# Index scratch in DRAM laid out by chunk, stored by groups of 32 partitions

## The reference, cut to what matters

```python
def _L0_ffn_ref(x, lut, gate_idx, up_idx, down_idx):   # lut: 16 values
    def _ghost_linear(x, idx, lut):
        w = lut[idx]
        return jnp.einsum('bsh,oh->bso', x, w)
    gate = _ghost_linear(x, gate_idx, lut)             # idx (1376, 512)
    up = _ghost_linear(x, up_idx, lut)                 # idx (1376, 512)
    h = jax.nn.silu(gate) * up
    return _ghost_linear(h, down_idx, lut)             # idx (512, 1376)
...
x = x + _L0_xattn_ref(_layernorm(x, axis=-1), ctx_1024, ...)
x = x + _L0_ffn_ref(_layernorm(x, axis=-1), L0_ffn_lut, ...)
```

## Time and profile before

| | |
|---|---|
| median of 3 executions | 803.66 us |
| the profiled execution | 803.88 us |
| its span | 802.1 us |
| TensorE busy | 752.2 us, 94% |
| VectorE busy | 518.6 us, 65% |
| ScalarE busy | 495.2 us, 62% |
| GpSimd busy | 265.2 us, 33% |
| moved by DMA | 61.49 MB in 75461 packets |

### The profile page before, as it was taken

How to read it: one execution, slowest core, us unless ns; L and a number is a source line. 1 busy time by engine, 2 the same in 40 slices (tenths; PEclk the granted TensorE clock), 3 DMA queues, 4 the chain that set the end, 5 groups by cost and what they waited for, 6 DMA issues and landing times.

```text
span 802.1 us, 14961 instructions
## 1 busy us (share of the span) xinstructions
PE 752.2 (94%) x5881; PEld 307.8 (38%) x5881; DVE 518.6 (65%) x1007; ACT 495.2 (62%) x1009; POOL 265.2 (33%) x276
## 2 busy tenths in 40 slices
PE   2887786999999999999999999999999999999998
PEld 1342232333443333224543332235433333265445
DVE  7979999899877994224879963228599810153221
ACT  3579889788556895662658866645489856511100
POOL 6883221000854322113843321035622310013320
PEclk9999999899999999999999999999999999999999
DMA  7649998596330000321400003222000000000001
GB/s 256 174 126 275 258 258 220 143 190 167 122 79 10 1 2 28 79 53 59 117 12 1 1 14 77 56 66 54 3 1 1 1 27 28 34 20 1 1 13 40
DMA packets 75461, 61.49 MB, mean 77 GB/s; under 512 B 34496, under 2 KB 61888, under 8 KB 75136
## 3 DMA queue, kind: packets, MB, share of 16 engines
q1 hardware_dynamic: 75056, 60.29, 28.3%
q10 hardware_dynamic: 208, 0.26, 0.1%
q0 software_dynamic: 128, 0.00, 0.0%
HBM read 43.55 MB, written 10.55 MB: 67 GB/s over the span
## 4 chain that ended last, share of the span: by engine, by line
PE 73%; DVE 16%; ACT 4%; issue 4%; POOL 3%; DVEq 0%; POOLq 0%; ACTq 0%
PE ps L1753 46%; PE ps L2120 8%; PE ps L2101 6%; PE ps L1819 5%; PE ps L2072 5%; DVE arena L1179 4%; DVE nmax L1548 3%; POOL hrstd L727 2%; ACT ps L1059 2%; PE ps L2107 2%; PE ps L1968 1%; DVE stat L1232 1%; DVE arena L1312 1%; DVE arena L1269 1%; DVE hvar L1302 1%
## 5 line engine op out<-in xcount | busy, mean ns | idle before, releaser
L1753 PE MATMUL ps<-arena,wf_hi 128*128 128x512 f16 (+1 forms) x704 | 201.4, 370 | 0.4 <-DVE arena L1192 0.4
L1059 ACT ACTIVATE ps<-ps,nmax 128x496 f32<-128x496 f32 x256 | 166.2, 652 | 23.1 <-DVE nmax L1553 23.1
L1091 ACT ACTIVATE arena<-ps 128x1024 f32<-128x1024 f32 x128 | 124.3, 1026 | 72.1 <-PE ps L2107 72.1
L1753 PE MATMUL ps<-arena,wf_lo 128*128 128x512 f16 (+1 forms) x352 | 130.0, 369 | 0.0
L1753 PE MATMUL ps<-wf_hi,arena 128*128 128x512 f16 (+3 forms) x374 | 114.8, 368 | 0.6 <-DVE arena L1196 0.6
L727 POOL TENSOR_TENSOR hrstd<-hvar,mhalf 128x16 f32<-128x16 f32 (+1 forms) x33 | 100.1, 3047 | 39.6 <-DVE hvar L1302 39.4
L1753 PEld LDWEIGHTS ps<-arena,wf_hi 128*128 128x128 f16 x704 | 64.7, 98 | 83.5 <-issue 20.5
L1179 DVE TENSOR_SCALAR arena<-arena,wf_lo 128x2048 f16<-128x2048 f16 (+1 forms) x132 | 89.6, 740 | 5.2 <-PE ps L1819 5.0
L1819 PE MATMUL ps<-arena,wf_lo 128*32 128x512 f16 (+1 forms) x1056 | 64.9, 389 | 13.0 <-ACT arena L886 9.6
L671 POOL TENSOR_TENSOR xrstd<-xvar,mhalf 128x1 f32<-128x1 f32 x32 | 24.0, 751 | 158.0 <-DVE xvar L1237 158.0
L1753 PE MATMUL ps<-wf_lo,arena 128*128 128x512 f16 (+3 forms) x187 | 68.5, 366 | 0.0
(11 more groups left out here) (164 smaller groups left out, 1051.6 us busy)
## 6 DMA issues: line engine op xcount, KB each, us to landing
arena<-idx SPq DMA_DIRECT2D x124, 128.0 KB, 3.5
arena<-in_x SPq DMA_DIRECT2D x32, 256.0 KB, 2.9
wf_lo<-in_idx SPq DMA_DIRECT2D x10, 512.0 KB, 5.1
idx<-wf_hi SPq DMA_DIRECT2D x10, 384.0 KB, 4.1
out<-arena SPq DMA_DIRECT2D x15, 256.0 KB, 2.0
wf_lo<-in_idx SPq DMA_DIRECT2D x11, 256.0 KB, 6.6
arena<-in_ctxT SPq DMA_DIRECT2D x5, 512.0 KB, 3.7
v_next<-arena SPq DMA_DIRECT2D x8, 256.0 KB, 4.2
```

The lines of the kernel that those rows point to most:

```text
L1059: last = act.activation(sc, sc, ACT.Exp, bias=nmax[:, 0, t, h:h + 1], accum_out=den[:, 0, t, h:h + 1])
L1091: act.activation(probs[n_ % 2][:, 2 * p:2 * p + 2, :], ps[:, bank:bank + 2, :], ACT.Exp).then_inc(s["probs_set"], 1)
L1753: last = pe.matmul(dst, l, r, start=(first and i == 0), stop=(stop and i == len(todo) - 1))
```

## The change

The scratch in DRAM becomes one flat array. Before, it had 128 rows, one for each partition, and a chunk was a column range of it, so that the four rows which one partition of a copy needs lay far apart: a piece of 1 KB each. Now a chunk is one range of the flat array, in the order k (32), g (4), column: what partition k of a copy needs is one piece of 4 KB (3 KB for the two short chunks). `load_rep` reads it so; it still issues four DMAs of 128 KB to 32 partitions each. For this the store must scatter: partition group g goes with one DMA of its own, in pieces of 1 KB that lie 4 KB apart. `store_idx` becomes 4 DMAs in place of 1 for blocks 1 to 10, and 8 in place of 1 for the short block, whose chunks have two widths. The first load of a block waits for all of them.

```diff
+def scratch_spans(it):
+
+    lo, mid, hi = block_at(it), down_at(it), block_at(it + 1)
+    return ((lo, mid, KQ * rows(it)), (mid, hi, D)) if it == SHORT else ((lo, hi, D),)
...
-        idx16 = nc.dram_tensor("idx16", (P, WCOLS), F16, kind="Internal").ap()
+        idx16 = nc.dram_tensor("idx16", (P * WCOLS,), F16, kind="Internal").ap()
...
             def store_idx(it):
-                cols = slice(block_at(it), block_at(it + 1))
                 sp.wait_ge(s["idx_16"], it + 1)
-                sp.dma_start(idx16[:, cols], wf_hi[:, cols]).then_inc(s[f"idx_out{it}"], 16)
+                for lo, hi, n in scratch_spans(it):
+                    for g in range(NR4):
+                        here = wf_hi[g * 32:(g + 1) * 32, lo:hi].rearrange("p (c n) -> p c n", n=n)
+                        there = idx16[P * lo:P * hi].rearrange("(c k g n) -> g k c n", k=32, g=NR4, n=n)[g]
+                        sp.dma_start(there, here).then_inc(s[f"idx_out{it}"], 16)
                 if it + STAGES < IT:
                     load_idx(it + STAGES)

             def load_rep(c):
                 lo, hi = CHUNKS[c]
                 if c % 3 == 0:
-                    sp.wait_ge(s[f"idx_out{c // 3}"], 16)
+                    sp.wait_ge(s[f"idx_out{c // 3}"], 16 * NR4 * len(scratch_spans(c // 3)))
...
-                src = idx16[:, lo:hi].rearrange("(g k) n -> k g n", g=NR4)
+                n = NR4 * (hi - lo)
+                src = idx16[P * lo:P * hi].rearrange("(k n) -> k n", k=32)
                 for r in range(NR4):
-                    dst = l_rep[c % REPS][r * 32:(r + 1) * 32, 0:NR4 * (hi - lo)].rearrange("p (g n) -> p g n", g=NR4)
-                    sp.dma_start(dst, src).then_inc(s[f"rep_in{c % REPS}"], 16)
+                    sp.dma_start(l_rep[c % REPS][r * 32:(r + 1) * 32, 0:NR4 * (hi - lo)], src).then_inc(s[f"rep_in{c % REPS}"], 16)
```

## The result

The changed kernel takes 805.42 us (median of 20 executions, 803.69 to 808.81), the kernel before 803.89 us in the same sessions (20, 802.47 to 806.49). The ratio is 1.0021, 95% interval 1.0013 to 1.0028: slower by 1.5 to 1.7 us, just at the size that I had called no change, and outside the range that I had given. The profiled execution took 806.06 us with a span of 804.2 us, 2.1 us more than the span before.

A forecast was written before the change was run, and what follows sets the result against it. The prediction took VectorE (58 to 142 us), then TensorE (to 204 us), as the bound, with DMA engines full but nobody waiting on the scratch. Its terms summed to 0, ends 0 and +0.5 us: 803.7 us, range 801.6 to 805.0.

The forecast's parts named there:

- the size that I had called no change: Whole run: differences up to about 0.2%, 1.6 us, count as no change; chance 0.82, own range 802.1 to 805.3 us.
- What bounds the kernel: Lookup, 58 to 204 us: VectorE until 142 us, then TensorE; DMA engines full, but only GpSimd waits for a DMA.
- The loads of 4 KB: The 132 replicated loads in 4 KB pieces: landing earlier gains 0 us, since nobody waits for them.
- the end "as now": Speed of the 4 KB loads: slow end, 2.65 us of DMA time a chunk, 198 GB/s; other end 1.39 us.
- The new wait for four stores: Chunk 3's load waits for block 1's four stores until 62.1 to 64.7 us; cost 0 us, 0.5 at the far end.
- The DMA engines' load: DMA time for two chunks: 7.6 to 11.05 us of 10.5; still hidden, share 0.72 to 1.0 from 58 to 142 us.
- the rival with a backlog: DMA engines fall behind, loads land late on VectorE in chunks 6 to 20: 11 us, 814.7 us; chance 0.05.
- The faster rival: Full DMA engines cost chain "issue" time from 58 to 142 us: 5.1 us would go, 798.6 us, half 801.1; chance 0.10.
- signs of being wrong: A DMA releasing the comparisons, chain "issue" shrinking by microseconds, or the comparisons' pace of 5.27 us a chunk moving.
- SP's additional stores: SP issues 37 more stores, 15.9 us, 1.3 us per two chunks in the loop; it fits, what queues behind is hidden.
- its second point: Index loads GpSimd waits for: conversion 5 moves from 81.83 to 83.1 us, ends at 84.6; hidden with 1.3 us left.
- My two slower rivals: DMA engines fall behind, 814.7 us, chance 0.05; chunk 3 starts late after its wait for stores, 805.5 us, chance 0.03.

The follow-up runs named there:

- one_store: Changed kernel with 4 KB loads, but host lays out index rows so each block is stored by one DMA of 128 partitions (two for the short block); 804.25 us, 1.0008.
- split_rows: Kernel before, old scratch and 1 KB loads, but each store issued as 4 DMAs of 32 partitions; 805.22 us, 1.0016.
- split_cols: Kernel before with each store issued as 4 DMAs, each a quarter of the columns on all 128 partitions; 805.67 us, 1.0029.
- idx_first: Changed kernel with the index load of block it + 2 issued before the four stores of block it instead of behind them; 804.32 us, 1.0008.
- conv5_inside: Kernel before, transfers untouched, but GpSimd's conversion 5 also waits for the first of the four comparisons of chunk 5; 805.83 us, 1.0033.
- conv5_behind: Changed kernel with GpSimd's conversion of block 5 put behind the two steps that followed it; 804.41 us, 1.0009.
- gated_after: Changed kernel with GpSimd's conversions of blocks 5, 9 and 10 moved to where VectorE compares nothing; 804.27 us, 1.0004.
- gated_idx_first: Changed kernel with the index load ahead of the stores and the conversions of blocks 5, 9 and 10 moved away from comparisons; 804.22 us, 0.9999.

## Why the prediction was wrong, by its own steps

**What bounds the kernel**: right. VectorE to 142 us and TensorE to 204 us are still the chain, and no comparison waits for a replicated load in the changed kernel. But from "the only engine that waits for a DMA is GpSimd" I drew that the transfer was slack. That wait was the one fed by SP.

**The loads of 4 KB**: right that nobody waits for them. As to speed the end "as now" held. In one_store, the loads of chunk 2 are alone between 42.5 and 46 us, as in the earlier trace rows; they ran at 204 GB/s against 198 with pieces of 1 KB:

```profile
42.50:46.00 3.50, 3.50 (x23) 2.37 (x23) 2.37 (x5) 2.94 (x6) 3.50 (x2) 1.00 0.88 204
```

So between the two rules of the Trainium skill, the one of "SBUF — State Buffer", Door 1: The DMA port swizzle (the rate follows from the ports that the partitions reach, half of them for 32 partitions) agrees, and the gain from 1 to 4 KB that "Perfetto Trace Analysis", DMA Optimizations, holds out did not come for this shape. The loads did not land sooner either. From 58 to 142 us they took 4.6 us in the median and 9.1 at most, against 4.1 and 7.0 in the earlier trace rows:

```profile
DMA to landing us min/median/max: 2.4/4.6/9.1
```

That goes with what SP issues ahead of them and not with the pieces: split_rows and split_cols, with pieces of 1 KB, have a median of 4.6 us too; one_store, with pieces of 4 KB, has 3.9, and idx_first, with four stores behind the index load, 3.5. The packet count was right within 600.

**The new wait for four stores**: right that it costs nothing. The forecast of 62 to 65 us was too late, as chunk 3's load was issued at 61.02 us, 0.3 us later than before; the scattered stores landed sooner than the whole one had (median 2.8 us against 4.4 in the earlier trace rows).

**The DMA engines' load**: right. The share from 58 to 142 us is 0.92, inside 0.72 to 1.0, and the rival with a backlog did not come. The faster rival is out too: "issue" in the chain of that stretch went up from 8.0% to 11.3%. One of the signs of being wrong did come: from chunk 3 to chunk 12 it is 5.56 us a chunk, not 5.27.

**SP's additional stores**: this is the step that failed, at its second point, the index loads that GpSimd waits for. I moved conversion 5 from 81.83 to 83.1 us with an unchanged duration and found 1.3 us left. What the profile shows in its place is a conversion that ends at 86.64 us, next steps of GpSimd that are late, and 2.6 us lost over chunks 5 and 6. Three things were wrong in it. First, I carried over only the issue time; in the profiled execution the landing was 1.0 us longer as well, and the conversion started at 84.26. Of the landing time I had taken one value as if it did not scatter. Second, 83.1 us already lay within the comparisons of chunk 5, which ran from 82.96 to 85.8 us, and I took a duration measured outside them (1.47 us) for one inside (2.38). The kernel's waits on `oh_set` put the conversions between the comparisons, and I read them as order only. Third, I asked how late GpSimd's next step would be, not what stood behind it. TensorE already idled 2.37 us there on ScalarE, which waited for GpSimd for 1.4 us; in the profiled execution it idled 1.1 us more and ran the next lookup at the lower clock, 1.5 us longer. How many of the 20 executions have that term is not shown; the 1.7 us between their two groups are near its size. My two slower rivals looked at the scratch, its backlog and its first wait, and neither at the index load behind the stores.

The chance of 0.08 for slower was too small for a change that adds 1.3 us of issue ahead of a transfer that someone waits for.

## What to carry to other kernels

An additional DMA issue is not priced at its own wait but at that of the next transfer on the same queue that somebody waits for; follow that one through every engine behind it. A wait that only keeps two engines apart in time is a schedule: what arrives 2 us late falls onto the other engine's work, and one of the two or both become slower. Where a change makes TensorE idle longer on a chain of handovers, add the lower clock for its next work as a possible term with a chance of its own, not as a sure one: here it came after waits of 3.05, 3.43 and 4.43 us and stayed away after 3.15 and 3.23. And where several executions fall into two groups, one profile speaks for one of them.

## What the runs showed of the hardware

- A conversion on GpSimd and comparisons on VectorE, both from SBUF to SBUF, hold each other up: the conversion takes 1.47 us alone and up to 2.38 beside comparisons, four comparisons 2.74 alone and up to 3.94. The Trainium skill, "SBUF — State Buffer", Who interferes with whom, says that GpSimd shares ports with VectorE's two-port modes, which `tensor_scalar` can enter, under an exclusive lock, and that the one which issues first makes the other wait. Two profiles agree with it. In the changed kernel the comparisons were first (82.58 us) and took 2.73 us, and the conversion (84.26) took 2.38. In one_store the conversion was first (82.71) and took 1.47 us, and the comparisons (82.98) took 3.73. In conv5_inside the conversion began among the comparisons and both paid: four comparisons grew by 1.2 us, the conversion by 0.45.
- The row maxima, which read PSUM, are not touched by this: the 31 of them from 58 to 142 us of the changed kernel take 1.175 to 1.192 us each, the 1.172 to 1.191 us of the kernel before, although conversions lie beside some of them.
- TensorE kept its clock at 1.00 after 2.37 us without work, and had 0.55 in the stretch after 3.43 us. Between these the outcome varied: 0.72 after 3.05 us (idx_first), 1.00 after 3.15 (conv5_inside) and after 3.23 (one_store).
- With four stores a block ahead of the index load the replicated loads landed after 4.6 us in the median (changed kernel, conv5_behind, gated_after, split_rows, split_cols), with one store after 3.8 to 4.2 us, whatever the pieces. With the four stores behind the index load it was 3.5 and 3.6 us (idx_first, gated_idx_first).
